# Expert loop four rounds deep instead of two, with the bias products behind the loop

## The reference, cut to what matters

```python
h = _L0_tok_ref(x, ...)
h = h + _L0_attn_ref(_layernorm(h), ...)
h = h + _L0_ffn_ref(_layernorm(h), ...)

def _L0_ffn_ref(x, Wr, br, W1, b1, W2, b2):
    logits = xf @ Wr + br
    topk_logits, topk_idx = jax.lax.top_k(logits, TOP_K)      # TOP_K = 2
    gates = jax.nn.softmax(topk_logits, axis=1)
    combine = zeros((T, E)).at[arange(T)[:, None], topk_idx].add(gates)
    for e in range(E):                                        # E = 64
        h = jax.nn.relu(xf @ W1[e] + b1[e])                   # 64 -> 128
        y = h @ W2[e] + b2[e]                                 # 128 -> 64
        out = out + combine[:, e:e + 1] * y
```

## Time and profile before

| | us |
|---|---|
| median of 3 runs | 826.35 (825.86 to 828.7) |
| the profiled execution | 826.82 |
| its span, first to last instruction | 825.0 |
| expert loop, first row transpose to first gather of the last share | 513.6 to 755.2 |
| gathers of the last share, on POOL | 755.2 to 815.7 |

### The profile page before, as it was taken

One profiled execution on the slowest core, in us unless ns is written; L12 is line 12 of the kernel. 1 busy time (PEld: TensorE's weight loads), 2 busy tenths in 40 slices (PEclk: granted clock), 3 DMA queues, 4 the chain that ended last, 5 costly groups with the idle time before them and its releaser, 6 DMA issues.

```text
span 825.0 us, 8871 instructions
## 1 busy us (share of the span) xinstructions
PE 487.8 (59%) x2520; PEld 315.3 (38%) x2520; DVE 559.5 (68%) x1180; ACT 319.5 (39%) x582; POOL 599.0 (73%) x393
## 2 busy tenths in 40 slices
PE   4835046468576557655784656877878886873000
PEld 4834012122122122222443233766667775763000
DVE  1597799999999999999774727345545463336211
ACT  2259856556556654552430311232323332330000
POOL 5986769999999999996056455466666636666774
PEclk9959567978879887979677666799999997997555
DMA  7999990000000000000035102488888897853211
GB/s 232 382 207 125 91 8 0 0 0 0 0 1 0 0 0 0 0 0 0 1 83 149 47 21 69 132 246 236 242 259 236 256 268 227 232 142 99 62 38 27
DMA packets 106604, 84.95 MB, mean 103 GB/s; under 512 B 30464, under 2 KB 90240, under 8 KB 106560
## 3 DMA queue, kind: packets, MB, share of 16 engines
q1 hardware_dynamic: 79312, 54.76, 30.8%
q10 hardware_dynamic: 19184, 21.40, 8.7%
q0 software_dynamic: 8064, 8.27, 4.1%
HBM read 57.22 MB, written 33.49 MB: 110 GB/s over the span
## 4 chain that ended last, share of the span: by engine, by line
POOL 31%; PE 29%; issue 16%; DVE 10%; ACT 5%; another core or an unknown queue 5%; SPq 1%; POOLq 0%; ACTq 0%; DMA 0%; DVEq 0%
POOL x_w L581 14%; POOL w_ring L574 10%; PE ps L906 9%; PE ps L897 6%; POOL xt L654 6%; PE ps L888 3%; PE ps L679 2%; PE ps L920 1%; PE ps L828 1%; DVE lstat L1282 1%; PE ps L668 1%; PE ps L770 1%; ACT xp L1096 1%; DVE lstat L1443 1%
## 5 line engine op out<-in xcount | busy, mean ns | idle before, releaser
L743 PE MATMUL ps<-x_w,ident 128*128 128x512 f32 x252 | 152.5, 762 | 102.2 <-POOL x_w L581 102.2
L633 POOL DMA_INDIRECT sorted_rows<-xp,slot_i x126 | 122.5, 972 | 103.3 <-issue 31.8
L654 POOL DMA_INDIRECT xt<-expert_out,slot_i x126 | 123.3, 978 | 70.7 <-issue 33.5
L574 POOL TENSOR_TENSOR w_ring<-xt,bc 128x2016 f32<-128x2016 f32 x32 | 144.3, 4510 | 13.4 <-DVE hh_ring L1411 7.3
L1411 DVE TENSOR_TENSOR_SCAN hh_ring<-ps,w_ring 128x1024 f32<-128x1024 f32 x64 | 145.9, 2279 | 0.1
L581 POOL TENSOR_TENSOR x_w<-hh_ring,bc 128x2016 f32<-128x2016 f32 (+1 forms) x32 | 141.8, 4436 | 0.0
L743 PEld LDWEIGHTS ps<-x_w,ident 128*128 128x128 f32 x252 | 59.6, 247 | 197.8 <-POOL x_w L581 125.7
L1066 ACT ACTIVATE ps<-dt_t,a_exp 128x1024 f32<-128x1024 f32 x64 | 71.5, 1117 | 63.8 <-DVE hh_ring L1411 63.8
L1060 ACT ACTIVATE ps<-dt_t,a_exp 128x1024 f32<-128x1024 f32 x64 | 71.6, 1118 | 51.0 <-DVE w_ring L1390 51.0
L1390 DVE TENSOR_TENSOR w_ring<-ps,w_ring 128x1008 f32<-128x1008 f32 x64 | 76.7, 1199 | 3.9 <-ACT ps L1060 3.9
L1405 DVE SCALAR_TENSOR_TENSOR w_ring<-ps,w_ring 128x1008 f32<-128x1008 f32 x64 | 75.6, 1182 | 0.0
(11 more groups left out here) (209 smaller groups left out, 903.4 us busy)
## 6 DMA issues: line engine op xcount, KB each, us to landing
dt_t<-packed SPq DMA_DIRECT2D x140, 96.5 KB
x_w<-packed SPq DMA_DIRECT2D x112, 96.5 KB
x_w<-sorted_rows ACTq DMA_DIRECT2D x40, 256.0 KB
expert_out<-x_w ACTq DMA_DIRECT2D x80, 128.0 KB
sorted_rows<-pad_rows SPq DMA_DIRECT2D x2, 3584.0 KB, 24.1
bc<-packed SPq DMA_DIRECT2D x68, 96.5 KB
packed<-in_L_ffn_W SPq DMA_DIRECT2D x3, 2048.0 KB, 42.2
x_w<-in_x SPq DMA_DIRECT2D x7, 448.0 KB, 8.9
```

Of the source, the lines that this page charges most:

```text
L574: pool.tensor_tensor(w_buf(k, 2), up3[:, bass.ds(c * DC, DC), 1:S].unsqueeze(1).broadcast_to([P, 2, DC, L]), vec_of(k, 2), ALU.mult).then_ ...
L633: pool.indirect_dma_start(out=sorted_rows[h], out_offset=bass.IndirectOffsetOnAxis(ap=slot_i[:, c, l:l + 1], axis=0), in_=xn[:, l, :], in_ ...
L654: pool.indirect_dma_start(out=y[:, l, :], out_offset=None, in_=expert_out[h], in_offset=bass.IndirectOffsetOnAxis(ap=slot_i[:, c, l:l + 1] ...
L743: ins = pe.matmul(ps[:, i, :], ident[:, :], src[:, i * BANK:(i + 1) * BANK], start=(k < 0), stop=(k == (N - 2 if last else N - 1)), skip_g ...
```

## The change

LAG_H becomes 4 and LATE 8: PE may start round k once ACT and DVE have finished round k - 4. The transposes are no longer made for a unit in every even round but for one step, two of them, in every round. `xT_e` and `hT_e` get four places (`hT_e` moves into `w_ring`), and the ring of weights has 25 places instead of 23. In PSUM each round has two banks, k % 4 and 4 + k % 4. The first holds the rows of round k (columns 0 to 255) and the hidden products of the even tiles (256 to 511), the second the hidden products of the odd tiles (0 to 255) and the output products (256 to 511). An output product still has 128 columns. Its first 64, which nobody reads, lie over the place of the tile before it, so the last tile is made first and each later product overwrites the unread half. DVE then copies 256 adjacent columns.

The bias chain leaves the loop. Behind the loop PE makes the 8 groups one after the other, with two places in PSUM and two in `cT`: transposes of group q, then the products of group q - 1. ACT copies behind its last store, and DVE adds ahead of the gated sums. POOL waits for these additions (`s_cbc`): at d = 212, 215, up to 233 for group 0, 1, up to 7.

```diff
-XRING = 8
+XRING = 10
 WRING = XRING + 15
-LAG_H, LATE = 2, 4
-TURNED, ADDED = 13, 15
+DEPTH = 4
+LAG_H, LATE = DEPTH, 2 * DEPTH
...
+BIAS_AT = {212 + 3 * q: q + 1 for q in range(CQ)}
...
+        def bank_of(k):
+            return ps[:, k % DEPTH, :], ps[:, DEPTH + k % DEPTH, :]
+
+        def rows_home(i, j, n=1):
+            return bank_of(i)[0][:, j * P:(j + n) * P]
+
+        def hidden_home(i, t, j):
+            return bank_of(i + LAG_H)[t][:, (2 * (1 - t) + j) * P:(2 * (1 - t) + j + 1) * P]
+
+        def outputs_home(i, a, z):
+            return bank_of(i + LATE)[1][:, 2 * P + a * C:2 * P + z * C]
...
                 if d in STEP_AT:
                     pool.wait_ge(s_pstep, STEP_AT[d] + LATE)
+                if d in BIAS_AT:
+                    pool.wait_ge(s_cbc, BIAS_AT[d])
...
             def outputs(i):
 
-                for j, n in enumerate(pairs_of(i)):
-                    for t in range(2):
-                        last = pe.matmul(ps[:, 6 + i % 2, (2 * j + t) * OUT:(2 * j + t + 1) * OUT], hT_e[:, i % 2, t, j, :],
+                for j, n in reversed(list(enumerate(pairs_of(i)))):
+                    for t in (1, 0):
+                        q = 2 * j + t
+                        last = pe.matmul(outputs_home(i, q - 1, q + 1), hT_e[:, i % DEPTH, t, j, :],
                                          w_of(n)[:, t, HID + C - OUT:HID + C], start=True, stop=True)
...
-            pe.wait_ge(s_b2, 32)
-            rows_T(0).then_inc(s_pstep, 2)
-            for k in range(2, STEP0[-1] + LATE):
-                pe.wait_ge(s_astep, k - LAG_H + 1)
+            for k in range(STEP0[-1] + LATE):
+                if k >= LAG_H:
+                    pe.wait_ge(s_astep, k - LAG_H + 1)
                 if k >= LATE:
                     pe.wait_ge(s_dstep, k - 2 * LAG_H + 1)
                     last = outputs(k - LATE)
-                if k < STEP0[-1] + LAG_H:
+                if LAG_H <= k < STEP0[-1] + LAG_H:
                     last = hidden(k - LAG_H)
-                if k % 2 == 0 and k < STEP0[-1]:
-                    last = rows_T(k // 2)
-                if group_at(k, TURNED) is not None:
-                    last = gates_T(group_at(k, TURNED))
-                if group_at(k, ADDED) is not None:
-                    last = bias_of(group_at(k, ADDED))
+                if k < STEP0[-1]:
+                    last = rows_T(k)
                 last.then_inc(s_pstep, 1)
+
+            pe.wait_ge(s_b2, 32)
+            pe.wait_ge(s_dstep, dve_rounds(STEP0[-1]))
+
+            def bias_of(q):
+
+                pe.wait_ge(s_cTc, q + 1)
+                if q >= 2:
+                    pe.wait_ge(s_cbc, q - 1)
...
+            for q in range(CQ):
+                pe.wait_ge(s_comb, q + 1)
+                if q >= 2:
+                    pe.wait_ge(s_cTc, q - 1)
...
+                last.then_inc(s_cT, 1)
+                if q > 0:
+                    bias_of(q - 1)
+            bias_of(CQ - 1)
...
             for i in range(STEP0[-1] + LAG_H - LATE - 1, STEP0[-1]):
                 store(i)
+
+            for q in range(CQ):
+                act.wait_ge(s_cT, q + 1)
+                if q >= 2:
+                    act.wait_ge(s_cb, q - 1)
+                act.activation(cT[:, q % 2, :], ps[:, q % 2, :], ACT.Copy).then_inc(s_cTc, 1)
...
+            for q in range(CQ):
+                n = min(8, L - 8 * q)
+                h = hg[:, 8 * q:8 * q + n, :]
+                dve.wait_ge(s_cb, q + 1)
+                ch.link(dve.tensor_tensor(h, ps[:, 4 + q % 2, 0:n * C].rearrange("p (l d) -> p l d", d=C), h, ALU.add))
+                dve.sem_inc(s_cbc, 1)
             for g in range(len(OUTS)):
```

More of the change, by code:

```diff
@@ L124, in groups_of @@
     return range(a // QG, -(-z // QG))
-def group_at(k, first):
-    return (k - first) // 8 if k >= first and (k - first) % 8 == 0 and (k - first) // 8 < CQ else None
 def dve_rounds(steps):
@@ L881, in _, with rows_T @@
             pe.wait_ge(s_tei, len(SHARES))
[L884 to L888 removed]
+            def rows_T(i):
+                for j, n in enumerate(pairs_of(i)):
+                    u = unit_of(n)
+                    if in_share(n) % UNIT == 0:
+                        pe.wait_ge(s_rows[u % RING], 16 * (u // RING + 1))
+                    last = pe.transpose(rows_home(i, j), rows_in[:, u % RING, in_share(n) % UNIT, :],
+                                        ident[:, :])
                 return last
@@ L1629, in _ @@
                     last = y_copy(k - LATE)
-                if group_at(k, ADDED) is not None:
-                    last = add_bias(group_at(k, ADDED))
                 last.then_inc(s_dstep, 1)
```

86 lines of the change are left out of this document (39 added, 47 removed).

## The result

| | before | after |
|---|---|---|
| median of 20 runs, us | 827.11 (821.63 to 834.36) | 824.82 (820.48 to 833.11) |
| the profiled execution, us | 826.82 | 825.59 |
| its span, us | 825.0 | 823.7 |
| d = 48 to d = 62 (start to start) | 25.7 | 27.3 |
| d = 62 to d = 158 | 156.2 | 152.3 |

A forecast was written before the change was run, and what follows sets the result against it. POOL and PE were taken to bound the kernel in a ping-pong, PE's signals being held during bursts of indirect DMAs. 826.8 - 6 - 4 + 2 + 7 = 825.8, median 0.5 lower: 825.4 us, range 816 to 835.

The forecast's parts named there:

- Steady loop, -6: Loop, d = 62 to 205: four rounds ahead let PE work through bursts of eight DMAs, -6 us (ends 0 and -14).
- rival (4): Loop: pause reading right, but bursts stay at four because DVE or a store holds PE; 833 us, chance 0.14 with (2).
- the merging: Loop: two POOL bursts of four DMAs become one of eight, gaining 0.34 us, 18 times.
- The reading of the longer stall: Stall at 687: ACT starts at 693.35, 5.4 us after PE's round, its signal held during POOL's eight DMAs.
- Wait for the stores, -4: POOL's pause at d = 158: four rounds signalled together shorten it by 4 us (ends 0 and -10.6).
- Head, +2: Loop start: added transposes and hidden steps before the first output product, with signals held, +2 us (0 to +4).
- Bias work leaving the loop, 0: Loop: PE is freed of 15 us of bias work but is not the longer side, so 0 us.
- The end of the loop: Loop's end at d = 206: forecast 8 us earlier, at 747.
- Behind the loop, +7: After d = 206: bias chain beside 46 gathers stops POOL three times, 3.0, 2.1 and 2.1 us, +7 us.
- The cover of DVE's gated sums: After d = 233: remaining 18 gathers (23 us) cover DVE's delayed gated sums, 3 us to spare; end stays 9.3 us.
- (1): Behind the loop: POOL stops at every third gather, eight stops of 13 to 34 us; 832 to 845 us, chance 0.14.
- (2): Loop: depth gives nothing because PE itself is late or DMA limits; only the chain adds, 833 us, 0.14 with rival (4).

The follow-up runs named there:

- e1: Kernel before, depth two, with only the bias chain moved behind the loop and POOL's waits for it; 833.25 us against 826.76, ratio 1.0087.
- e3: Changed kernel with POOL waiting for PE only at every fourth old stop in the loop, forcing bursts of eight; 853.43 us, ratio 1.033.
- e8: Forced bursts of eight as in e3, with only one of four output products made per step, so results are incomplete; 820.11 us in a single run.
- e7: Kernel before, depth two, with POOL beginning its gathers only when the expert loop is through; 894.69 us in a single run.
- e2: Changed kernel without POOL's waits for the bias sums, nothing computed left out; 844.89 us, ratio 1.0228.
- e12: Changed kernel run once more without an edit, on a third chip; 831.43 us against 831.98 for the kernel before, ratio 1.001.
- e5: Changed kernel with each of the first share's 32 gathers replaced by two fills on POOL, that output not computed; 812.15 us in a single run.
- e6: Changed kernel with POOL beginning its gathers only when the expert loop is through; 891.55 us in a single run.
- e9: Changed kernel at depth three instead of four, on another chip; 753.91 us, ratio 1.0001 to the kernel before, which took 753.47 beside it.
- e11: Kernel before at depth three, bias chain in the loop, POOL's pace raised to 88 steps in 153 DMAs; 754.34 us, ratio 1.0013.

## Why the prediction came out right, and where it did not

**The total** was right (825.4 predicted, 824.82), but in part by luck. The sum had the loop 6 + 4 - 2 = 8 us shorter and the chain 7 longer, -1 together. Against the kernel before, the trace has the loop 1.5 us shorter (-3.2 from d = 62 to 206, +1.7 ahead of it) and 3.6 more behind it, +2.1 together; two errors of 6.5 and 3.4 us went opposite ways, and 3.4 us in unchanged code did the rest in the profiled pair. Against e1, where the two halves are apart, the depth gave 7.1 us between d = 62 and 206, 5.3 with the head, and the chain alone cost 7 (0.87% of 826.8).

**Steady loop, -6: the step failed.** The step was that with four rounds ahead "PE works on through a burst of eight DMAs". It does not: it is held itself, in the third round of a burst of four (570.60 and 572.03 in the trace of after) and in the fourth of a burst of eight (e3). Bursts stayed at four, as rival (4) said in its outcome but not in its reason (it named DVE or a store). From d = 62 to the end of d = 157 the gain is 0.95 us (144.4 against 145.3). From d = 158 to the end of d = 205 it is 2.7 us, which the longer wait at d = 206 (4.86 against 1.45) more than takes back. The 10 us that the sum had between d = 62 and 206 came out as 3.2 against before, 7.1 against e1. And e8 suggests that the merging is worth 3.8 us ahead of d = 158 where it works, most of which the wait there takes back. The two terms of the sum were not independent: the share of POOL and the stores of PE end at the same place, and the later one counts.

The kernel before could not have shown it. "Only the signals are held" and "PE is held as well" give the same ping-pong at depth two, where PE has nothing to do after two rounds, and part at depth four. The row of 562.91 in the earlier trace rows looks like a clue, with 1.42 us of "issue", but it is the first product of a round and waits for DVE's answer (`s_dstep`). DVE's copy of the round that counts ends at 562.68, 0.23 us ahead of it:

```profile
562.27 0.41 DVE L1596 COPY x_w<-ps 128x256 f32<-128x256 f32 x1
```

No output product of the three traces at depth two (before, e1, e7) is preceded by a stop inside its round.

The reading of the longer stall was off in one place. The row of 693.35 in the earlier trace rows is ACT's copy of the gates, the answer to the round before the one that ends at 687.90. The transposes of that earlier round (the gates, line 913) run from 684.93 to 685.59, so its signal was 7.8 us late and not 5.4; the two signals came together all the same.

**Wait for the stores, -4: right in size**, measured -3.0 (7.89 against 10.86; 7.74 in e2 and 7.66 in e12). Its reason, four rounds signalled together, is not what happened: ACT still learns of two rounds at a time. Which part of the deeper order shortens the wait was not isolated.

**Head, +2: not settled.** d = 62 starts 9.84 us after the burst ahead of it instead of 8.12 us, +1.7. But in the other traces at depth four that wait is between 5.8 us (e5) and 11.2 (e12), though nothing ahead of it differs, and at depth two it is 8.1 in all three.

**Bias work leaving the loop, 0: right**, by e1 (156.3 us against 156.2 to d = 158). **The end of the loop** was forecast at 747; d = 206 starts at 750.33, 4.9 us earlier than before, of which 3.4 lie ahead of d = 48. The longer wait at d = 206 that comes with the chain behind (e1) was not in the sum.

**Behind the loop, +7: mis-sized, +3.6.** I had three stops of 3.0, 2.1 and 2.1 us; there is one, of 4.65 - 0.30 = 4.35 us. The gaps of DVE's bias sums show why: a signal in the course of a burst is slow, not stopped, so that five groups came through without a stop. The rest of the difference is that the gathers themselves are a little faster where DVE is idle beside them: 46 of them take 57.5 us in e2 and 60.4 in the kernel before. The cover of DVE's gated sums held (the end stays 9.3 us after the last gather), and e2 shows how thin the construction is: without the stops the kernel is about 18 us longer.

**The rivals.** (1), a stop at every third gather, did not happen; one or two did. Its price was also added up wrongly: 13 to 34 us instead of 7 give 831 to 852, not 832 to 845. (2) said that PE is late itself, and that is half right, but then the depth was to give nothing, and it gave 7.1 us in the loop against e1. The Trainium skill (Perfetto Trace Analysis, Summary: the profiler window per engine type) says that the end shown for TensorE is an estimate; what decides here are recorded starts, 570.60 and 572.03, which that page leaves standing, so the trace of the changed kernel settles it.

**The mechanism** is known up to this point: indirect DMAs in a row hold up PE's signals, the more the longer the burst, and after two rounds (bursts of four) or three (bursts of eight) PE; fills on POOL do not (e5), and without the DMAs a round takes 2.0 us (e6). It was in force in eleven of the fourteen traces and absent in the three of e9 to e11, in which an indirect DMA takes 0.97 us with 0.30 between two, as everywhere. Those three ran on another chip than e1 to e8 and e12, in one session, so whether it hangs on the chip or on the moment is open. What shares the way between POOL's descriptors and PE's signals was not found. The Trainium skill (NOTIFIC — the notification-queue block, 7.1 Overflow) says that the block that writes the records of instructions can hold back its producers, which would be one candidate; no run here shows it.

## What to carry to other kernels

Idle time of TensorE with the cause "issue", in the middle of a group of matmuls that waits for nothing, is a result and not noise; at the head of a group, where the code waits, it is more often a wait that the profile failed to name. In the first case ask what was running on the other engines, and hold it against a stretch in which that is absent. Before deepening a pipeline, find out whether the engine waits for an answer or is itself stopped, for depth helps only against the first, and look for a second wait (here the stores at d = 158) that takes the gain back. Put work that needs several handovers where nobody issues indirect DMAs back to back, or make the issuer stop for it: the stop of 4.4 us saved about 18. And measure a change of half a per cent in more than one session: a condition that differed between sessions was worth 9% here, and with it absent none of the variants differed from the kernel before; the changed kernel itself was not run there.

## What the runs showed of the hardware that was not expected

- TensorE can be stopped, in mid-group and without a wait, by GpSimd's indirect DMAs: one or two matmul records for each DMA of 1.26 us from some point of a burst on. That point came after 26 to 40 records in bursts of four (changed kernel) and 53 to 60 in bursts of eight (e3), or 36 to 44 where a round has 12 records and not 18 (e8).
- The delay of a TensorE signal grows within a burst of indirect DMAs, from under 0.5 us in the first 5 us to 20 us for one sent 34 us into the burst (e2). In the loop the held signals arrive about 1 us after GpSimd stops (571.12, then ACT at 572.11).
- All of it can be absent. On the same kernel before, 29 runs in one session took 750.6 to 759.0 us and the runs of the other sessions 821.6 to 836.3.
- Beside fills of 128x512 on GpSimd a tensor_scalar of 128x64 takes 505 ns on VectorE instead of 309.
